# A layer kernel on one core: the weights that stream in 256 columns start at 320 modulo 512 in their partitions instead of at 0

## The reference

```python
xn = layernorm(x)
# attention without softmax, 16 heads of 16
q = elu(xn @ Wq + bq) + 1 ;  k = elu(xn @ Wk + bk) + 1 ;  v = xn @ Wv + bv
kv = sum_k k^T v ;  att = (q @ kv) / max(q . sum k, 1e-6) @ Wo + bo
# shared expert, and 8 routed experts of which each token takes 2
shared = swiglu(xn @ w_in.T) @ w_out.T            # 256 -> 2*512 -> 256
h      = swiglu(xn @ w1.T)                        # one first layer for all experts
routed = sum over the token's 2 experts e of  weight_e * (h @ w2[e].T)
out = x + att + shared + routed
```

## Time and profile before

| what | value |
|---|---|
| median of 3 runs | 922.63 us |
| the profiled execution | 922.05 us, of which the span from first to last instruction is 920.2 us |
| matmuls of TensorE (PE) | 903.5 us busy, 98% of the span |
| weight loads (PEld) | 815.6 us, 89% |
| VectorE, ScalarE, GpSimd | 694.1, 367.3 and 403.9 us |

### The profile page before, as it was taken

How to read it: one execution, slowest core, us unless ns; L and a number is a source line. 1 busy time by engine, 2 the same in 40 slices (tenths; PEclk the granted TensorE clock), 3 DMA queues, 4 the chain that set the end, 5 groups by cost and what they waited for, 6 DMA issues and landing times. The chain is left out here.

```text
span 920.2 us, 22781 instructions
## 1 busy us (share of the span) xinstructions
PE 903.5 (98%) x6982; PEld 815.6 (89%) x6983; DVE 694.1 (75%) x1816; ACT 367.3 (40%) x605; POOL 403.9 (44%) x486
## 2 busy tenths in 40 slices
PE   8999999999999999999999999999999999999996
PEld 7798988889898989888898989898888999999996
DVE  6878777787868687777878696877676777777773
ACT  5654544353545445443525454453432222222220
POOL 3654342443425243424434243434242666555554
PEclk9999999999999999999999999999999999999999
DMA  6432413132322324141323223241156888888870
GB/s 216 136 116 70 125 51 120 69 103 90 93 100 93 116 69 125 46 125 69 103 80 103 91 92 126 69 125 47 59 204 144 145 143 143 148 137 135 137 128 1
DMA packets 141992, 98.63 MB, mean 107 GB/s; under 512 B 53136, under 2 KB 133008, under 8 KB 141968
## 3 DMA queue, kind: packets, MB, share of 16 engines
q1 hardware_dynamic: 103584, 62.50, 23.7%
q0 software_dynamic: 15920, 25.32, 12.5%
q10 hardware_dynamic: 22464, 10.51, 4.8%
HBM read 53.29 MB, written 46.43 MB: 108 GB/s over the span
## 5 line engine op out<-in xcount | busy, mean ns | idle before, releaser
L350 PE MATMUL bank<-wexp_hi,xnT_hi 128*128 (+1 forms) x560 | 188.1, 336 | 1.5 <-DVE xnT_lo L1149 1.1
L352 PE MATMUL bank<-wexp_hi,xnT_lo 128*128 (+1 forms) x560 | 185.7, 332 | 0.0
L351 PE MATMUL bank<-wexp_lo,xnT_hi 128*128 (+1 forms) x560 | 185.7, 332 | 0.0
L1227 POOL TENSOR_TENSOR h_lo<-gated,h_hi 128x256 fp32r<-128x256 f32 x128 | 98.7, 792 | 141.2 <-ACT h_hi L709 141.2
L350 PEld LDWEIGHTS bank<-wexp_hi,xnT_hi 128*128 128x128 f32 x560 | 106.3, 190 | 15.1 <-issue 4.6
L352 PEld LDWEIGHTS bank<-wexp_hi,xnT_lo 128*128 128x128 f32 x560 | 106.4, 190 | 10.3
L351 PEld LDWEIGHTS bank<-wexp_lo,xnT_hi 128*128 128x128 f32 x560 | 106.4, 190 | 9.5
L350 PE MATMUL bank<-xnT_hi,win_hi 128*128 128x512 f32 x256 | 102.1, 399 | 0.0
L351 PE MATMUL bank<-xnT_lo,win_hi 128*128 128x512 f32 x256 | 100.4, 392 | 0.0
L352 PE MATMUL bank<-xnT_hi,win_lo 128*128 128x512 f32 x256 | 99.6, 389 | 0.0
L1251 POOL TENSOR_TENSOR res<-res,bo_t 128x256 f32<-128x256 f32 x64 | 49.2, 801 | 112.3 <-DMA res<-x 112.3
(11 more groups left out here) (198 smaller groups left out, 2377.4 us busy)
## 6 DMA issues: line engine op xcount, KB each, us to landing
res<-x SPq DMA_DIRECT2D x16, 512.0 KB, 3.6
out<-res SPq DMA_DIRECT2D x16, 512.0 KB, 2.8
xt<-x SPq DMA_DIRECT2D x15, 512.0 KB, 3.4
xn_d<-xt SPq DMA_DIRECT2D x15, 512.0 KB, 4.9
xt<-xn_d SPq DMA_DIRECT2D x60, 128.0 KB, 2.7
xt<-h_d SPq DMA_DIRECT2D x76, 64.0 KB
xt<-h_d ACTq DMA_DIRECT2D x76, 64.0 KB
kb<-h_d SPq DMA_DIRECT2D x76, 64.0 KB
```

The lines of the kernel that those rows point to most:

```text
L350: e.matmul(to, w_hi, m_hi_, start=first_, stop=False, skip_group_check=free)
L351: e.matmul(to, w_hi, m_lo_, start=False, stop=False, skip_group_check=free)
L352: return e.matmul(to, w_lo, m_hi_, start=False, stop=last_, skip_group_check=free)
L1227: ins = pool.tensor_tensor(h_lo[:, j, cols], gated[:, j % 2, cols], h_hi[:, j, cols].bitcast(f32), ALU.subtract)
```

## The change

Three things, and none of them adds, removes or moves an instruction. `wexp` loses its first 2048 columns, which become a buffer of their own (`wone`) at 0 modulo 512. `wexp`, `wout`, `wv` and `m` are allocated first of all, behind a margin of 192 instead of 384 bytes, and so start at 320 modulo 512; their three narrow high parts stand together, and then the three low parts. A filler of 192 bytes (`aside`) brings what follows back to 0. So before and after:

| operand | start modulo 512 before | after | low part behind its high part before | after |
|---|---|---|---|---|
| `wexp`, second layer | 0 | 320 | 40,960 bytes | 32,768 bytes |
| `wout` | 0 | 320 | 4,096 | 8,192 |
| `wv`, `m` | 0 | 320 | 2,048 | 8,192 |
| first expert layer, `wq`, `win`, `xnT`, `h`, `qn` | 0 | 0 | | |
| `wk` | 0, 128 and 256, 384 | the same | | |

Everything from `wo` to `h_lo` moves up by 4,096 bytes; what was allocated behind `m` stays where it was.

```diff
         KL = D + 10
-        LINE = 512
-        CONSTS = 128
-        sb("margin", [P, (LINE - CONSTS) // 4], f32)
-        wv_hi, wv_lo = pair("wv", [P, DC, D])
+        SHIFT = 192
+        sb("margin", [P, SHIFT // 4], f32)
+        wexp_hi, wexp_lo = pair("wexp", [P, B * UNIT])
+
+        def narrow(part):
+            return (sb("wout_" + part, [P, HC, D], f32r), sb("wv_" + part, [P, DC, D], f32r),
+                    sb("m_" + part, [P, DC, D], f32r))
+
+        wout_hi, wv_hi, m_hi = narrow("hi")
+        wout_lo, wv_lo, m_lo = narrow("lo")
+        sb("aside", [P, SHIFT // 4], f32)
+        wone_hi, wone_lo = pair("wone", [P, W1])
         wq_hi, wq_lo = pair("wq", [P, DC, D])
         win_hi, win_lo = pair("win", [P, DC, 1024])
-        wout_hi, wout_lo = pair("wout", [P, HC, D])
-        wexp_hi, wexp_lo = pair("wexp", [P, W1 + B * UNIT])
         wo = sb("wo", [P, DC, D], f32)
...
-        m_hi, m_lo = pair("m", [P, DC, D])
...
-            w1_hi = wexp_hi[:, 0:W1].rearrange("p (c n) -> p c n", c=DC)
-            w1_lo = wexp_lo[:, 0:W1].rearrange("p (c n) -> p c n", c=DC)
+            w1_hi = wone_hi[:, :].rearrange("p (c n) -> p c n", c=DC)
+            w1_lo = wone_lo[:, :].rearrange("p (c n) -> p c n", c=DC)
...
-                            off = at[n] + (W1 + j * D)
+                            off = at[n] + j * D
...
-                    split(b, b * UNIT + W1, UNIT)
+                    split(b, b * UNIT, UNIT)
```

More of the change, by code:

```diff
@@ L335, in layer_program @@
         w1_parts = [wstage[:, :], flat(gated)]
-        stage_w1 = [(w1_parts[n], w_exp[:, n * 1024:(n + 1) * 1024], wexp_hi[:, n * 1024:(n + 1) * 1024],
-                     wexp_lo[:, n * 1024:(n + 1) * 1024]) for n in range(2)]
+        stage_w1 = [(w1_parts[n], w_exp[:, n * 1024:(n + 1) * 1024], wone_hi[:, n * 1024:(n + 1) * 1024],
+                     wone_lo[:, n * 1024:(n + 1) * 1024]) for n in range(2)]
         stage_out = [(by_chunk(wstage[:, :], D), w_out, wout_hi[:, :, :], wout_lo[:, :, :])]
@@ L1277, in batch @@
                     biased()
-                    split(0, W1, UNIT)
+                    split(0, 0, UNIT)
             reciprocal_root(0)
```

## The result

The changed kernel takes 916.51 us (median of 4 runs, 915.42 to 917.56) beside 922.79 (922.33 to 923.48). The ratio is 0.9936, with a 95% interval of 0.9923 to 0.9948: 6.3 us between the medians, and by the ratio 0.64% faster. The forecast was 916.0 us.

What follows compares the result with a forecast made beforehand. TensorE, its matmuls busy 903.5 of 920.2 us, was taken as the bound. Savings of 6.5 and 0.2 us, together 6.7, off 922.05 give 915.4; with 0.6 for the median, 916.0 us, range 900 to 925.

Steps and rivals of the forecast that it cites:

- The distances: In wexp, wout and m, the start of 320 takes 2.2 ns off each of 2952 matmuls: 6.5 us.
- The start can move a distance: In wk's second chunk, from 128 and 384, matmuls took 2.5 ns less, so a stream's start moves its distance.
- A lasting state, with other states near it: In long stretches, 120.0 ns is a state a stream from 0 falls into and keeps; preceding streams can delay it.
- `wv` and the changes of form: In batches: wv gains 0.5 ns on 384 matmuls, 0.2 us; matmuls behind form changes shift up to 1.0 us, either sign.
- Low parts behind high, other addresses, first expert layer: New high-to-low distances, the 4,096-byte move and the separate first expert layer, still from 0: costed at nothing.
- Does it reach the end?: Whole kernel: VectorE leaves 0.7 us a tile, the likeliest case asks for 0.05, so the full 6.7 us arrives.
- No change: All touched streams: the weight load itself costs the 13.3 ns whatever the start; 922.6 us, chance 0.15.
- Slower: All 3336 touched matmuls: 320 is a worse start, 2.5 to 3 ns more each; 930.9 to 932.6 us, chance 0.22.
- The short distance of 113.3: Touched streams settle at y's short first distance, saving 6.7 ns on 2952 and 5.0 per wv; 901.0 us, chance 0.23.
- The estimate of 109.2 ns: Touched streams: the skill's N / 2.4 + 2.5 ns for 256 columns; if reached, an estimated 35 us saved.

Runs made afterwards that it cites:

- the scan: Single executions of the changed kernel with other starts for wexp, for wout, wv and m, and in some for the first expert layer; 915.82 to 921.30 us.
- e1_pairs_320: Changed kernel with each low part right behind its high part again, all still starting at 320 modulo 512; 916.39 us, ratio 0.9935.
- e2_low_behind_0: Changed kernel's order of buffers, but with all streams starting at 0 modulo 512; 922.17 us, ratio 1.0001.
- e3_all_320: Changed kernel with everything behind the constants 320 bytes later, stationary operands and wk as well; 922.53 us, ratio 1.0009.
- e12_others_480: Changed kernel with the 256-column streams back at 0 modulo 512 and everything else at 480; 915.10 us, ratio 0.9929.
- e7_parts_apart: Changed kernel with wexp's high part from 0 and low from 320, and wout, wv and m the other way; 921.30 us.
- e11_all_32: Changed kernel with wexp, wout, wv and m all from 32 modulo 512; 914.15 us, ratio 0.9916 to the kernel before.
- e8_scan_32_96: Changed kernel with wexp from 32 modulo 512 and wout, wv and m from 96; 918.61 us in one execution.

## Why the prediction was right, step by step

**The distances.** The forecast took 2.2 ns off each of 2952 matmuls in `wexp`, `wout` and `m`. It is 2.22 in `wexp` (120.0 to 117.78) and the same in y's steady part: 2952 x 2.22 = 6.55 us where the forecast had 6.5 for them. Over the whole of y it is a little less, 0.15 us in each of 16 batches, since its first distance was a short one before. The choice between 1.7 and 2.5 was a choice between rows, and hit by some luck: at other differences the scan gives 0 to 3.3.

**The start can move a distance.** This rested on the 2.5 ns that the second chunk of `wk` took less. The direction was right, and e1_pairs_320 and e2_low_behind_0 show that such a dependence is there. But the prediction spoke of the stream's own start, and e3_all_320 and e12_others_480 show that it is the start against that of what else is read, by the load under each matmul most likely the stationary operand. With every stationary operand at 0 in the kernel before, the two come to the same number, so the forecast did not suffer. The sample was weaker evidence than it looked: 128 gives 120.0 ns once a stream runs long from it. In K and V no stream is steady, and the steps that the prediction set beside each other carry what came before them.

**A lasting state, with other states near it.** Right, and it turned out to be the core of it. Two unequal averages at one and the same difference (e12_others_480) and the patterns of e7_parts_apart show it.

**`wv` and the changes of form.** The forecast was 0.5 ns for `wv` and up to 1.0 us of either sign for the changes of form. Over the four tiles of the batch `wv` gained 0.8 ns, and the `wk` between lost 1.3, most of it in the six matmuls behind y (0.76 us for 0.74). Together +0.01 us a batch, 0.2 us in all: inside the bound, but `wk` did not keep its steps as the text expected.

**Low parts behind high, other addresses, first expert layer.** Costed at nothing; e1_pairs_320 and e2_low_behind_0 show nothing for the first two, and the wone row still has 389 ns where the 512 columns stayed at 0.

**Does it reach the end?** Yes in the medians: 1800 x 2.22 and 16 x 0.15 are 6.4 us, less 0.2 for K and V is 6.2, and the medians lie 6.3 apart. The profiled execution came out at 917.56, 1 us over the median, with the 1.6 us of the half clock in it.

**The rivals.** No change falls. Here the Trainium skill, SBUF — State Buffer, section Who interferes with whom, has TensorE's two read ports as independent, so that it never waits: the trace does not agree, since e2_low_behind_0 and e12_others_480 run the same instructions on the same streams and differ by 3.3 ns a matmul, with nothing moved but where everything else starts. Slower falls for 320; no difference tried made a long stream of 256 columns slower than 120.0 on average. That rival stood on 291 ns against 288 in `wk`, whose low part starts at 256 and 384. Long streams from there take 120.0 and 118.7, so these starts are not slow ones. Why the low part's mean stays the larger one next to its high part (289 against 287 in e11_all_32) is open. The short distance of 113.3 does not last at any of the thirteen differences: it comes as one step in four of a pattern whose average is 116.7, the least (e8_scan_32_96, e11_all_32). The estimate of 109.2 ns from the Trainium skill, TensorE: Matmul & The Clock Gate, section Back-to-back issue gap, was reached nowhere at the full clock. The section gives its formula for a single matmul by itself, and here a load runs under each.

**What stays open.** That two reads of the same memory meet in some bank is still my picture of it. The runs show that the difference of the starts sets the average, that it repeats at 256 bytes in the three pairs tried on the same buffers, that 16 bytes already matter, and that what remains of the overhead is 10 of 13.3 ns at best. They also show it gone at the half clock (below), so it is no fixed price of a load. They show no bank and no rule that would give the values of the table, and no run moves the stationary operands alone.

## What to carry to other kernels

When TensorE is the bound and its distances are longer than its columns, move the streamed operand by 32, 64, ... bytes against the stationary one and read the distance in the profile: one profile can try a different start in each stage, and here that showed more than reasoning did. Look at the steady distance in long stretches, and at the whole batch, since a good start for one stream can disturb its neighbours (96: K and V 5.84 us in place of 5.79), and columns of another number may want another start. Buffers that are allocated one behind the other with sizes that are powers of two all start alike, and at a difference of 0 this kernel's 256 columns had the slowest steady pace of the table, with 96, 128 and 256.

## What the runs showed of the hardware

**The distance is set by the difference of two addresses.** 256 float32r columns with a weight load under each matmul: 120.0 ns on average at a difference of 0 or 256, 116.7 at 32 or 288. Moving the streams by 32 (e11_all_32) or all the rest (e12_others_480) gives the same average, and moving everything by 320 (e3_all_320) gives 120.0 again.

**The overhead is gone at the half clock.** Starts in the 3.4 us at the 1.2 GHz level, in the profile after (difference 320, 14 distances) and in that of e12_others_480 (difference 32, 13 distances):

```profile
694.40 0.41 PE L355 MATMUL bank<-wexp_hi,xnT_hi 128*128 x1
...
697.39 0.41 PE L357 MATMUL bank<-wexp_hi,xnT_lo 128*128 x1
```

```profile
692.01 0.41 PE L366 MATMUL bank<-wexp_hi,xnT_lo 128*128 x1
...
694.78 0.39 PE L364 MATMUL bank<-wexp_hi,xnT_hi 128*128 x1
```

2.99 / 14 and 2.77 / 13 are 213.6 and 213.1 ns, and 256 / 1.2 is 213.3. Nothing is left beside the columns, at either difference. In the profile before the first `wv` matmuls, at 12 us, run at the same level from a difference of 0: six take 1.28 us, 213.3 ns. At the full clock the same streams take 10 to 13.3 ns more than their columns.

**Paces lock, and can lock twice.** In all runs the steady steps repeat to the nanosecond over hundreds of matmuls, but for a matmul held up now and then, whatever the DMA and the other engines do. They are equal or a pattern of a few. At a difference of 32 there are two steady paces, 117.8 ns (three tiles in e12_others_480) and 116.7 ns, and with one held-up matmul the stream went from one to the other.

**A half clock in some of the profiles.** In the profile after, 2.29 us lie between the starts of the last matmul of the batches and the first of the second expert layer. TensorE then ran nine matmuls and had its clock at 0.50, the 1.2 GHz level, for 3.4 us. Before, the same gap was 1.43 us and the clock stayed at 1.00. In e12_others_480 the same happened behind a gap of 2.10 us, in e8_scan_32_96 a gap of 2.31 us passed without it. Here it costs 1.6 us, a quarter of what the change brings. The profiled execution has a mean clock of 0.993 and the other three of the changed kernel 0.995 to 0.996, so it is likely theirs lack it; they have no trace.
